# Batch 2's split and first query chunk, and the work of tiles 22 and 23, reordered in a cross-attention and FFN kernel

## What is computed

```python
def reference(x, ctx_768, Wq, Wk, Wv, Wo, bo, clip_x, clip_down, w_gate, w_up, w_down):
    # attention with 8 heads of 64 over the 77 context rows of the same batch
    q, k, v = layernorm(x) @ Wq, ctx_768 @ Wk, ctx_768 @ Wv
    attn = softmax(q @ k.T / 8)                 # per head
    x = x + (attn @ v) @ Wo + bo
    # feed-forward with fake-quantized activations (one scale over the whole tensor) and weights
    xq = act_fake_quant(layernorm(x), clip_x)
    gate, up = xq @ weight_fake_quant(w_gate).T, xq @ weight_fake_quant(w_up).T
    h = act_fake_quant(silu(gate) * up, clip_down)
    return x + h @ weight_fake_quant(w_down).T
```

## Time and profile before

| | |
|---|---|
| median of three runs | 535.89 us |
| the profiled execution | 535.88 us, span 534.1 us |
| TensorE (PE) busy | 524.1 us, 98% |
| VectorE (DVE) busy | 449.2 us, 84% |
| ScalarE (ACT) busy | 289.8 us, 54% |
| GpSimd (POOL) busy | 230.1 us, 43% |

### The profile page before, as it was taken

One profiled execution on the slowest core, in us unless ns is written; L12 is line 12 of the kernel. 1 busy time (PEld: TensorE's weight loads), 2 busy tenths in 40 slices (PEclk: granted clock), 3 DMA queues, 4 the chain that ended last, 5 costly groups with the idle time before them and its releaser, 6 DMA issues.

```text
span 534.1 us, 7958 instructions
## 1 busy us (share of the span) xinstructions
PE 524.1 (98%) x2717; PEld 354.1 (66%) x2724; DVE 449.2 (84%) x812; ACT 289.8 (54%) x417; POOL 230.1 (43%) x349
## 2 busy tenths in 40 slices
PE   8999999999999999999999999999999999999997
PEld 7888688787888888888778644444444445444444
DVE  4966898989989899898899679998999988777663
ACT  4844656565465655554435745545554543999300
POOL 4396679689596876866453000000000000055332
PEclk9999999999999999999999999999999999999999
DMA  8818465846667565435959964942243020499997
GB/s 311 291 79 293 120 167 188 289 150 217 219 201 243 188 226 182 158 110 174 214 88 337 259 187 190 324 118 41 79 119 91 29 39 19 176 334 207 135 111 122
DMA packets 82941, 93.81 MB, mean 176 GB/s; under 512 B 47085, under 2 KB 50157, under 8 KB 82645
## 3 DMA queue, kind: packets, MB, share of 16 engines
q1 hardware_dynamic: 77877, 84.13, 51.2%
q0 software_dynamic: 4320, 7.87, 9.9%
q10 hardware_dynamic: 704, 1.31, 0.8%
HBM read 47.51 MB, written 37.78 MB: 160 GB/s over the span
## 4 chain that ended last, share of the span: by engine, by line
PE 86%; DVE 6%; POOL 2%; DMA 2%; ACT 1%; issue 1%; SPq 0%; DVEq 0%; ACTq 0%; POOLq 0%
PE QO L613 14%; PE SP L618 14%; PE SP L419 6%; PE QO L335 4%; PE QO L333 4%; PE QO L334 4%; PE SP L665 4%; PE PTP L665 4%; PE QO L665 4%; PE PTP L452 3%; PE WOP L490 2%; PE WOP L492 2%; PE WOP L491 2%; PE MI L492 2%; PE MI L490 2%; PE MI L491 2%
## 5 line engine op out<-in xcount | busy, mean ns | idle before, releaser
L1570 POOL DMA_DIRECT2D out<-n2b x30 | 28.0, 975 | 205.6 <-DVE n2b L1389 205.5
L904 ACT ACTIVATE sil<-QO,fsc 128x512 f32<-128x512 f32 x87 | 59.8, 687 | 71.5 <-PE QO L613 70.9
L613 PE MATMUL QO<-nT,wgu 128*128 128x512 bf16 x340 | 87.3, 379 | 0.1
L618 PE MATMUL SP<-nT,wgu 128*128 128x512 bf16 x340 | 87.3, 379 | 0.0
L1332 DVE SCALAR_TENSOR_TENSOR h<-SP,fsc,sil 128x512 f32<-128x512 f32 x87 | 65.3, 750 | 16.7 <-PE SP L618 13.8
L1471 POOL TENSOR_TENSOR PN<-P,rs 128x512 f32<-128x512 f32 x64 | 44.2, 713 | 43.4 <-DVE rs L988 43.4
L1338 DVE TENSOR_REDUCE hmx<-h 128x1 f32<-128x512 f32 (+1 forms) x89 | 60.1, 679 | 2.9
L618 PEld LDWEIGHTS SP<-nT,wgu 128*128 128x128 bf16 x340 | 33.2, 98 | 40.2 <-DVE h L1332 0.3
L613 PEld LDWEIGHTS QO<-nT,wgu 128*128 128x128 bf16 x340 | 33.2, 98 | 40.2 <-ACT sil L904 0.3
L727 ACT ACTIVATE P<-P,r 128x616 f32<-128x616 f32 x32 | 26.0, 811 | 50.0 <-DVE P L979 50.0
L935 ACT ACTIVATE h<-h,g 128x1536 int8<-128x1536 f32 (+2 forms) x38 | 44.3, 1257 | 0.0
(11 more groups left out here) (230 smaller groups left out, 1204.2 us busy)
## 6 DMA issues: line engine op xcount, KB each, us to landing
xTr<-in_xT SPq DMA_DIRECT2D x8, 1024.0 KB, 7.7
xn<-in_x SPq DMA_DIRECT2D x32, 256.0 KB, 4.2
out<-x SPq DMA_DIRECT2D x32, 256.0 KB, 3.1
n_rows<-n SPq DMA_DIRECT2D x32, 256.0 KB, 2.9
n2b<-n_rows SPq DMA_DIRECT2D x32, 256.0 KB, 3.7
out<-n2b POOLq DMA_DIRECT2D x30, 256.0 KB, 5.6
h_spill<-h SPq DMA_DIRECT2D x2, 2816.0 KB, 8.2
h<-h_spill SPq DMA_DIRECT2D x6, 768.0 KB, 6.7
```

The costliest lines, as they stand in the source:

```text
L613: mm = e.matmul(QO[:, at:at + 512], wgu_v[:, k, cols(ic)], nT[:, b % 2, :, k, :], start=(k == 0), stop=(k == 3))
L618: mm = e.matmul(SP[:, at:at + 512], wgu_v[:, k, cols(NI + ic)], nT[:, b % 2, :, k, :], start=(k == 0), stop=(k == 3))
L904: e.activation(sil[:, n % SR, :], QO[:, (n % 2) * 512:(n % 2) * 512 + 512], ACT.Silu, scale=fsc[:, ic:ic + 1]).then_inc(silu, 1)
```

## The change

Batch 2's `split_hi` waits for each k until the last chunk of batch 1 has used that k (semaphore `xT_used`). Its low halves are shared out as 1, 3 on GpSimd and 0, 2 on VectorE, and moved in all programs. Query chunk (2,0) goes to the bank MI and leaves `QO_USES`, so the other uses after it swap banks, and PV(0,1) waits for v_rows(4) in its place; wo(1), the next user of MI, waits for the copy. v_rows(4) goes ahead of S(4). SP issues load_xT(2) before load_xn(4). In wo(23) the heads 2, 3, 0 are multiplied where all four were, and head 1 after PT(28); ScalarE's first three os copies of batch 6 wait for the first part, the fourth for the second. normed(22) goes behind PV_high(6) and PT_high(28), and residual(23) and second_stats(23) behind PV_low(6).

```diff
-        QO_USES += [("q", 1, m) for m in range(4)] + [("v", 4), ("q", 2, 0)]
+        QO_USES += [("q", 1, m) for m in range(4)] + [("v", 4)]
...
+            if use == ("q", 2, 0):
+                return MI[:, :]
...
-        LO_POOL = {0: (), 1: (1, 3), 2: (0, 1)}
-        LO_DVE = {0: (0, 1, 2, 3), 1: (0, 2), 2: (2, 3)}
+        LO_POOL = {0: (), 1: (1, 3), 2: (1, 3)}
+        LO_DVE = {0: (0, 1, 2, 3), 1: (0, 2), 2: (0, 2)}
...
                 # q_chunk, after each k's third matmul
+                    if m == 3 and k < 3:
+                        mm.then_inc(xT_used, 1)
...
+            def wo_pairs(n, js, first, last):
+                b, t = n // 4, n % 4
+                for j in js:
+                    w.wait_ge(os_lo, pv_count(b, j) if b == 7 else pv_count(b, 1))
+                    e.matmul(wo_bank(n), os_[:, 0, j, cols(t)], wos[:, 0, j, :], start=(j == first), stop=False)
+                    e.matmul(wo_bank(n), os_[:, 0, j, cols(t)], wos[:, 1, j, :], start=False, stop=False)
+                    mm = e.matmul(wo_bank(n), os_[:, 1, j, cols(t)], wos[:, 0, j, :], start=False, stop=(j == last))
+                return mm
...
             PT(2)
+            v_rows(4)
             S(4)
-            v_rows(4)
             PT(3)
             q_ahead(2)
...
-            wo(23)
+            w.wait_ge(x1_, 22)
+            wo_pairs(23, PV_ORDER[6][:3], PV_ORDER[6][0], 1).then_inc(wo_most, 1)
             PV_all(6)
             PT(28)
+            wo_pairs(23, PV_ORDER[6][3:], PV_ORDER[6][0], 1).then_inc(wo_mm, 1)
             S(29)
...
             # ScalarE, split_hi
-                w.wait_ge(q_mm, 4 * b)
+                if k < 3:
+                    w.wait_ge(xT_used, 3 * (b - 1) + k + 1)
+                else:
+                    w.wait_ge(q_mm, 4 * b)
...
             # ScalarE, PV_high
-                    w.wait_ge(wo_mm, 4 * b)
+                    if b == 6 and j != PV_ORDER[6][3]:
+                        w.wait_ge(wo_mm, 23)
+                        w.wait_ge(wo_most, 1)
+                    else:
+                        w.wait_ge(wo_mm, 4 * b)
...
             q_copy(1, 2)
+            split_hi(2, 0)
+            soft_exp(3)
+            split_hi(2, 1)
             q_copy(1, 3)
-            soft_exp(3)
-            split_hi(2, 0)
-            split_hi(2, 1)
             PT_high(2)
             split_hi(2, 2)
             split_hi(2, 3)
+            v_high(4)
             w_round(1)
-            v_high(4)
...
-            normed(22)
             PV_high(6)
             PT_high(28)
+            normed(22)
...
             # VectorE
             soft_sub(3)
+            split_lo(2, 0)
+            soft_sum(3)
+            soft_rec(3)
             w_top(1)
-            soft_sum(3)
             w_scale(1)
-            soft_rec(3)
             w_inverse(1)
-            soft_max(4)
             PT_low(2)
-            soft_sub(4)
             split_lo(2, 2)
             v_low(4)
-            split_lo(2, 3)
+            soft_max(4)
+            soft_sub(4)
             PT_low(3)
...
+            PV_low(6)
+            soft_max(29)
+            soft_sub(29)
             residual(23)
-            PV_low(6)
+            soft_max(30)
+            soft_sub(30)
             second_stats(23)
             second_aggr(23)
-            soft_max(29)
-            soft_sub(29)
-            soft_max(30)
-            soft_sub(30)
             PT_low(28)
...
             # GpSimd
             first_bias(4)
+            split_lo(2, 1)
             soft_norm(3)
-            split_lo(2)
+            split_lo(2, 3)
...
             # SP
+            load_xT(2)
             for n in range(4, XR):
                 load_xn(n)
             load_w(0)
-            load_xT(2)
```

More of the change, by code:

```diff
@@ L160, in block_kernel @@
         ct_hi, wk_hi, wq_hi, xT_hi, wv_hi, wo_hi = [sem(s) for s in ("ct_hi", "wk_hi", "wq_hi", "xT_hi", "wv_hi", "wo_hi")]
+        wo_most = sem("wo_most")
+        xT_used = sem("xT_used")
         ct_lo, wk_lo, wv_lo, wo_lo = [sem(s) for s in ("ct_lo", "wk_lo", "wv_lo", "wo_lo")]
@@ L274, in pv_bank @@
             return qo_bank("pv", b, j) if j < 2 else SP[:, (j - 2) * 512:(j - 2) * 512 + 512]
-        LO_POOL = {0: (), 1: (1, 3), 2: (0, 1)}
-        LO_DVE = {0: (0, 1, 2, 3), 1: (0, 2), 2: (2, 3)}
+        LO_POOL = {0: (), 1: (1, 3), 2: (1, 3)}
+        LO_DVE = {0: (0, 1, 2, 3), 1: (0, 2), 2: (0, 2)}
         for b_ in range(3, NB):
             LO_POOL[b_], LO_DVE[b_] = (0, 1, 2), (3,)
-        LO_ORDER = {1: (0, 1, 2, 3), **{b_: (0, 2, 1, 3) if b_ == 2 else (0, 1, 2, 3) for b_ in range(2, NB)}}
         def lo_pool_count(b):
@@ L390, in q_chunk @@
                 w.wait_ge(xT_lo_dve, lo_dve_count(b))
-                three(qo_bank("q", b, m), q_pairs(m)).then_inc(q_mm, 1)
+                bank, pairs = qo_bank("q", b, m), q_pairs(m)
+                for k in range(4):
+                    e.matmul(bank, pairs[k][0], pairs[k][2], start=(k == 0), stop=False)
+                    e.matmul(bank, pairs[k][0], pairs[k][3], start=False, stop=False)
+                    mm = e.matmul(bank, pairs[k][1], pairs[k][2], start=False, stop=(k == 3))
+                    if m == 3 and k < 3:
+                        mm.then_inc(xT_used, 1)
+                mm.then_inc(q_mm, 1)
             def q_ahead(b):
                 bank, pairs = qo_bank("q", b, 0), q_pairs(0)
-                wait_qo_free(w, "q", b, 0)
+                if b != 2:
+                    wait_qo_free(w, "q", b, 0)
                 for k in range(4):
@@ L400, in q_ahead @@
                     e.matmul(bank, pairs[k][1], pairs[k][2], start=False, stop=False)
-                for k in LO_ORDER[b]:
+                for k in range(4):
                     w.wait_ge(xT_lo_pool, lo_pool_count(b - 1) + sum(i <= k for i in LO_POOL[b]))
                     w.wait_ge(xT_lo_dve, lo_dve_count(b - 1) + sum(i <= k for i in LO_DVE[b]))
-                    mm = e.matmul(bank, pairs[k][0], pairs[k][3], start=False, stop=(k == LO_ORDER[b][-1]))
+                    mm = e.matmul(bank, pairs[k][0], pairs[k][3], start=False, stop=(k == 3))
                 mm.then_inc(q_mm, 1)
@@ L477, in PV_all @@
                     PV(b, j)
+            def wo_pairs(n, js, first, last):
[6 more added lines that the diff above has]
+                return mm
             def wo(n):
-                b, t = n // 4, n % 4
                 w.wait_ge(wo_lo, 1)
+                if n == 1:
+                    w.wait_ge(q_out, 9)
                 if n == 30:
@@ L487, in wo @@
                     w.wait_ge(x1_, n - 1)
[L488 to L493, removed]
+                wo_pairs(n, range(4), 0, 3).then_inc(wo_mm, 1)
             def keep_clock(n):
```

## The result

The changed kernel takes 540.01 us (median of 4 runs, 539.13 to 540.46), the kernel before 536.1 in the same session. The ratio is 1.0067, with a 95% interval of 1.0054 to 1.0081: slower by 3.6 us by that ratio, and 3.9 between the medians. The forecast was 537.1, in a range from 534.5 to 538.0; the direction was right, the time lies outside.

What follows compares the result with a forecast made beforehand. TensorE, busy 524.1 of 534.1 us, was taken as the bound, so only its waits count. Stretch A's +1.05 and stretch B's +0.1 gave +1.15, say 1.2, on 535.88: 537.1 us, range 534.5 to 538.0.

Steps and rivals of the forecast that it cites:

- The load: SP's queue: load_xT(2) moved ahead makes w(0) late, so PT(2) stalls 1.8 us and PT(3) another 0.9.
- I take 3.3: Lateness of w(0) in us, chosen by the landing of xT(2), between 2.9 and 3.4.
- The upper bound of 3.4: Most that w(0) could be late in us: seven transfers ending at 53.05, against 49.6 before.
- GpSimd's two steps: Before PT(3): first_bias(4) taken at 1.28 us and soft_norm(3) at 1.38, so PT(3) starts at 61.7.
- The upper end: PV_rest(0) later by +1.5 us if three of GpSimd's long operations each take 0.15 longer.
- The gain of the rest of A: 55 to 64 us: without any stall, the edits make the stretch 1.7 us shorter.
- rival 3: PV_rest(0) waits for PT_low(3), as VectorE's list has only 0.3 us of cover; +2 us, 537.9; chance 0.1.
- Stretch B: 254 to 270 us, wo(23) and batch 6's os copies: +0.1 us, bounds -0.5 to +0.3.
- -0.5 + 0.6 = +0.1: Before wo(26): fourth os low half ends 0.5 us earlier, residual(23), 0.6, now stands behind it.
- The middle: PV_rest(0) to S(25): loads move along with finished work, so no further change beyond the carried +1.05 us.
- I carry the +1.05 through batches 1 to 6: PV_rest(0) starts 1.05 us later, and everything behind it on all engines shifts with it.
- stretch A: 55 to 64 us, PT(2) to PV_rest(0): PV_rest(0) starts at 65.15 in place of 64.10, +1.05 us.

Runs made afterwards that it cites:

- e2: The kernel before with load_xT(2) ahead of load_xn(4), nothing else; 538.05 us.
- e3: The changed kernel with everything of stretch B undone; 537.71 us.
- e5: The changed kernel with PV_low(6) given the same split waits as PV_high(6); 538.90 us.
- e8: The changed kernel with GpSimd's soft_norm(3) ahead of split_lo(2,1); 539.46 us.
- e15: The changed kernel with VectorE's split_lo(2,2) behind v_low(4) and soft_max(4); 539.11 us.
- e1: The changed kernel with load_xT(2) back behind load_w(0), nothing else undone; 536.51 us.
- e4: The changed kernel with load_xT(2) back behind load_w(0) and all of stretch B undone; 535.05 us.
- e6: e7 with VectorE's changed tail order added, residual(23) behind PV_low(6) and soft_sub(29); 535.17 us.
- e7: e4, but with normed(22) kept behind PV_high(6) and PT_high(28); 534.59 us.
- e10: e7 with GpSimd's soft_norm(3) ahead of split_lo(2,1); 534.66 us.
- e9: The changed kernel, early load kept, with w(0)'s steps later: VectorE's behind soft_sub(3), w_round(0) behind split_hi(2,1), w_integer(0) behind split_lo(2,1); 536.30 us.
- e12: The changed kernel with SP's order load_w(0), load_xT(2), load_xn(4..8); 536.13 us.
- e13: e7 with SP's order load_w(0), load_xT(2), load_xn(4..8); 534.41 us.
- e14: The changed kernel with SP's order load_xn(4..8), load_xT(2), load_w(0); 540.23 us.

## Why the prediction was off

- **The load (right, 0.6 us short).** That w(0) would be late, that w_top(0) stands for it without slack, that PT_low(1) and so PT(2) follow, and then PT(3) for soft_norm(3): all four rows are there. "I take 3.3" was the term: counted from PT(1) it is 3.9 us, and the means of the six profiles with the early load and the six with the old place differ by 3.9 too. The upper bound of 3.4 took the old landing of xT(2) for the end of all seven transfers. Counted from PT(1), w_top(0) starts between 4.35 and 5.90 us with the early load (changed, e2, e3, e5, e8, e15) and between 0.79 and 2.24 with the old place (before, e1, e4, e6, e7, e10), though all run the same up to there. The landing scatters by 1.5 us, and the range had to hold that.
- **GpSimd's two steps (0.9 us short).** first_bias(4) was taken at 1.28 and soft_norm(3) at 1.38, from rows where no subtraction of two SBUF tiles ran beside them. They took 1.75 and 1.83, since VectorE's subtractions now fall on them. The upper end allowed 0.45 for three operations, not for each. PT(3) was forecast at 61.7 and came at 62.86 (63.05 from the same PT(1)); 0.6 and 0.9 more than account for this.
- **The gain of the rest of A (right in kind, short in size).** 1.7 us was forecast for the case without the late load; e1, e4 and e9 show 1.4 to 1.5, e6, e7 and e10 0.8 to 1.3, and e12, with w(0) first, 1.9. In e4, e6 and e10 PV_rest(0) waits 0.3 to 0.7 us for PT_low(3), which is the mechanism of rival 3.
- **Stretch B (the step that failed).** "VectorE halves three of the four from 256.9 to 258.9" is wrong: all four wait for the end of wo(23). I had read PV_high's new wait and not that PV_low keeps the old one. The step cost 1.6 us where 0.1 stood. With that wait split, in e5, the sum of the forecast, -0.5 + 0.6 = +0.1, is measured as +0.1. This step alone doesn't bring the miss: e5's median, 538.90, is still above 538.0.
- **The middle (not settled).** "I carry the +1.05 through batches 1 to 6" left out 0.7 us. Kernels with stretch A's edits show 165.7 to 166.6 there, those without (before and e2) 165.6. In the changed kernel 0.5 of the 0.7 lies between S(20) and S(22), where VectorE waits for a load of xn, ahead of the first low half before S(21), as the kernel before does not:

```profile
195.78 0.69 DVE L1028 BATCH_NORM_STATS2 bn<-xn 128x6 f32<-128x512 f32 x1 [0.41 <-DMA xn<-in_x]
```

The edits do not bring this wait by themselves. e3, e5 and e12 have them without it, and take 165.7 to 165.8; in e6, e7, e9, e10, e13, e14 and e15 it comes two batches earlier, near 130 us, with 0.4 to 0.8 us lost there. In e4, e6, e8 and e10 0.5 us lies right behind PV_rest(0), where S(5) waits for VectorE's os halves. Why a load of xn is late in one kernel and not in another was not separated.

The terms measured are -0.2 + 2.4 + 0.7 + 1.6 = 4.5 us between the two profiles; 3.9 between the medians. Against the forecast's +1.05 and +0.1, stretch A misses by 1.35, the middle by 0.7 and stretch B by 1.5.

## What to carry to other kernels

A load that an engine already waits for has no slack, so a larger load put ahead of it in the same queue is paid by everything behind the waiting step, less the slack that it has: look for what is queued behind that step, and either move the step (e9) or issue the small load first (e12). When one wait is split into two, search the code for every wait on the same semaphore and value; the one that is left as it was decides. And work that lies in an engine's idle gap is free only there: moved behind the wait that made the gap, it costs its full length.

## What the runs showed of the hardware

A GpSimd operation on SBUF took about 0.45 us more when VectorE's subtraction of two SBUF tiles (`xTs<-xTr,xTs`) was already running. The bias addition, in the kernel before and in the changed one (count, then ns minimum/median/maximum):

```profile
L1462 POOL TENSOR_TENSOR xn<-xn,bob x32: 1280/1297/1308, 44.8 to 274.6; 128x512 f32<-128x512 f32 x32
```

```profile
L1487 POOL TENSOR_TENSOR xn<-xn,bob x32: 1272/1294/1752, 44.6 to 279.3; 128x512 f32<-128x512 f32 x32
```

All 32 are alike before; after, a single one is 1752 ns long, the one beside split_lo(2,0). soft_norm(3), which is two operations, is 1.83 where split_lo(2,2) begins inside the first and runs into the second, and 1.38 beside PT_low(2), which reads one operand from PSUM (e15). Where GpSimd's operation began first, VectorE's split was the longer one: 0.68 at its shortest, 1.06 in the changed kernel, 1.65 in e8. In e10 it starts 0.03 us behind the bias addition, which keeps its 1.30:

```profile
54.03 1.30 POOL L1481 TENSOR_TENSOR xn<-xn,bob 128x512 f32<-128x512 f32 x1
54.06 1.82 DVE L962 TENSOR_TENSOR xTs<-xTr,xTs 128x512 fp32r<-128x512 f32 x1
```

The Trainium skill (SBUF — State Buffer, SBUF: two separate sides) states such an exclusion for a VectorE operation with two SBUF inputs against a GpSimd one that reads SBUF, the first to start having the port for its whole length; these lengths agree with it.

TensorE's clock fell in three of the sixteen profiles, e2, e5 and e8, each time behind the wait before PT(2) (2.40, 2.77 and 2.56 us), to 0.50 to 0.61 of full speed for 3 to 4.4 us. In the changed kernel's profile, with a wait of 2.34 us, it stayed at 1.00, but two of its four timed executions show a mean of 0.997. What the fall costs depends on what TensorE would wait for next: about 1.3 us in e2 by its timed executions, next to nothing in e5's profile, where it lay ahead of a wait.
